# Two Mamba layers as one run of 32 chunks, with weights exchanged on the way and the carries' constants copied by DMA

## What is computed

```python
def _block(x, in_w, cw, cb, xp_w, dtw, dtb, a_log, dp, ow):
    xb, z = jnp.split(jnp.einsum('bld,ed->ble', x, in_w), 2, axis=-1)
    xb = silu(conv of 4 taps over xb + cb)
    dbc = jnp.einsum('ble,re->blr', xb, xp_w)          # delta (16), Bm (16), Cm (16)
    delta = softplus(jnp.einsum('blr,er->ble', delta, dtw) + dtb)
    dA = jnp.exp(delta[..., None] * -jnp.exp(a_log))
    mi = delta[..., None] * Bm[:, :, None, :] * xb[..., None]
    def scan_fn(carry, inp):
        h, v = carry
        v = 0.6 * v + mi_t
        h = dA_t * h + v
        return ((h, v), einsum('ben,bn->be', h, C_t))
    y = (ys + dp * xb) * silu(z)
    return jnp.einsum('ble,de->bld', y, ow)
for i in range(2):
    x = x + _block(_rmsnorm(x, norm_w[i]), in_proj_w[i], ...)
```

## Time and profile before

| | |
|---|---|
| runs | 4176.25 us median of 3 (4171.02 to 4178.72) |
| profiled execution | 4180.98 us, its span 4179.2 us |
| mean granted TensorE clock | 0.863 of full speed |
| Mamba's two layers, first load to last residual | 974.7 to 3408.3 us of the span |
| first to last scan | 1065.0 to 2172.9 us, and 2283.1 to 3396.4 us |

### The profile page before, as it was taken

How to read it: one execution, slowest core, us unless ns; L and a number is a source line. 1 busy time by engine, 2 the same in 40 slices (tenths; PEclk the granted TensorE clock), 3 DMA queues, 4 the chain that set the end, 5 groups by cost and what they waited for, 6 DMA issues and landing times. The chain is left out here.

```text
span 4179.2 us, 94211 instructions
## 1 busy us (share of the span) xinstructions
PE 3158.1 (76%) x31116; PEld 2527.5 (60%) x31117; DVE 2746.0 (66%) x4803; ACT 2019.3 (48%) x4522; POOL 1996.0 (48%) x1170
## 2 busy tenths in 40 slices
PE   6888886991778888787864787787878753799980
PEld 4455554660666666676762676676667653688870
DVE  3444442325788888888874888887888877555445
ACT  1211211222676777677644777676676743133320
POOL 0100100001577777777661767767686766221116
PEclk8788886995889999999986899999999875799995
DMA  1000000002223232323221222323232324111113
GB/s 53 0 0 0 0 0 22 0 0 67 68 56 83 54 84 55 81 57 82 54 56 49 67 72 56 83 54 82 55 80 58 79 89 165 54 45 48 48 42 109
DMA packets 151643, 230.75 MB, mean 55 GB/s; under 512 B 25106, under 2 KB 83890, under 8 KB 149556
## 3 DMA queue, kind: packets, MB, share of 16 engines
q1 hardware_dynamic: 143156, 202.30, 18.1%
q0 software_dynamic: 8064, 23.08, 1.9%
HBM read 119.99 MB, written 23.59 MB: 34 GB/s over the span
## 5 line engine op out<-in xcount | busy, mean ns | idle before, releaser
L890 POOL TENSOR_TENSOR m_hc<-m_h,m_Cb 128x1024 f32<-128x1024 f32 x512 | 1230.1, 2410 | 627.4 <-DVE m_h L1014 366.6
L1014 DVE TENSOR_TENSOR_SCAN m_h<-m_dA,m_hlast,m_bank 128x256 f32<-128x256 f32 x2048 | 1344.8, 725 | 192.1 <-PE m_bank L1329 127.8
L1308 PE MATMUL m_bank<-ident,m_hc 128*128 128x128 f32 x4096 | 687.6, 297 | 298.1 <-POOL m_hc L890 297.8
L1152 ACT ACTIVATE m_dA<-m_delta,m_rate 128x256 f32<-128x256 f32 x2048 | 894.1, 500 | 15.7 <-issue 14.2
L1327 PE MATMUL m_bank<-m_M,m_U 128*128 128x64 bf16 x8192 | 688.4, 198 | 115.3 <-DMA m_U<-m_clo 92.1
L1327 PEld LDWEIGHTS m_bank<-m_M,m_U 128*128 128x128 bf16 x8192 | 615.9, 102 | 203.2 <-issue 141.3
L1329 PE MATMUL m_bank<-m_M,m_U 112*128 112x64 bf16 x8192 | 688.2, 198 | 5.2 <-issue 5.2
L1308 PEld LDWEIGHTS m_bank<-ident,m_hc 128*128 128x128 f32 x4096 | 473.9, 151 | 317.1 <-issue 316.8
L1329 PEld LDWEIGHTS m_bank<-m_M,m_U 112*128 112x128 bf16 x8192 | 588.2, 101 | 72.3 <-issue 51.1
L1995 ACT ACTIVATE x_h<-x_bank,x_b 128x256 f32<-128x256 f32 x320 | 134.4, 471 | 286.8 <-PE x_bank L1941 271.4
L1901 POOL DMA_INDIRECT x_x_in<-xn_rows,r_from_row x80 | 91.0, 1137 | 350.7 <-PE x_bank L1925 302.7
(11 more groups left out here) (279 smaller groups left out, 5990.2 us busy)
## 6 DMA issues: line engine op xcount, KB each, us to landing
m_Cb<-m_c_rows SPq DMA_DIRECT2D x256, 256.0 KB, 3.3
m_M<-m_Mhi SPq DMA_DIRECT2D x128, 256.0 KB, 4.3
m_M<-m_Mlo SPq DMA_DIRECT2D x64, 256.0 KB, 3.6
m_U<-m_Uhi SPq DMA_DIRECT2D x128, 128.0 KB, 3.1
y_rows<-x_y SPq DMA_DIRECT2D x40, 256.0 KB, 2.1
m_U<-m_Ulo SPq DMA_DIRECT2D x64, 128.0 KB, 3.1
g_stage<-in_e_w SPq DMA_DIRECT2D x8, 1024.0 KB, 5.2
o_stage<-in_e_w SPq DMA_DIRECT2D x16, 512.0 KB, 4.6
```

Source lines behind the costliest of these rows:

```text
L890: nc.gpsimd.tensor_tensor(hc[:, hc_slot[n]], h[:, n % RING], Cb[:, g % 2, n % NG, :].unsqueeze(1).broadcast_to([P, KI, CM]), ALU.mult).the ...
L1014: nc.vector.tensor_tensor_scan(h[:, n % RING, m, :], dA[:, n % RING, m, :], VB[(n % 2) * 2 + g][:, (m % 2) * CM:(m % 2 + 1) * CM], hlast[: ...
L1152: nc.scalar.activation(dA[:, n % RING, m, :], delta[:, par, m, :], ACT.Exp, scale=rate[:, m, n:n + 1]).then_inc(s["da_done"], 1)
L1308: last = nc.tensor.matmul(Y[half][:, m * P:(m + 1) * P], hc[:, hc_slot[n], m, half * P:(half + 1) * P], net.ident[:], is_transpose=True, s ...
```

## The change

`mamba_phase` runs once, for both layers: 32 chunks, where chunk 16 is the first of layer 1.

- Small per-layer weights (norm, taps, bias, rates, skip and its diagonals) are kept for both layers. The large ones (`w_in`, 1 MB, `w_xp`, `w_dt`) have one place: SyncE loads those of layer 1 in chunk 14, after its sixth spread and the placements of u, once the last products with the old ones are counted; TensorE waits for them (`swapped`) ahead of the input product of chunk 16. `w_out` is exchanged likewise in chunk 16, and waited for in chunk 17.
- Where layer 1 begins, the conv history is zeroed on GpSimd instead of copied (chunk 16), the last h of chunk 15 is kept as zeros on ScalarE, and VectorE fills the velocity's carry with zeros in chunk 15.
- Chunks 14 to 17 stand between two loops, written out on all engines. The slots' numbers go into a table `AT`, with the values that the code had.
- The six loads of the constants come first and on a semaphore of their own. VectorE makes one place of M2 and no longer waits for the other loads to do so; one transfer from SyncE's queue copies it to the other seven. TensorE waits for the copy ahead of the first velocity, and for the diagonals (now eight, a third `const_done`) ahead of its clearing.
- Each tap on VectorE adds one to a counted semaphore `tap_done` and waits for the tap before it there, instead of on a plain semaphore that was cleared at each chunk's start; likewise `joined` for the sum of delta.

```diff
-def mamba_phase(net, layer, xm):
+def mamba_phase(net, xm):
...
-        LOADS = 18 * 16
+        LOADS = (6 + 5 * LAYERS) * 16
+        LAST = LAYERS * NCM
...
-                for t, key in ((norm, "norm"), (w_in, "in"), (conv, "conv"), (conv_b, "conv_b"), (w_xp, "xp"),
-                               (rate, "alog"), (skip, "skip"), (w_out, "out")):
-                    sp.dma_start(t[:], dram[f"m{layer}_{key}"]).then_inc(s["loaded"], 16)
-                sp.dma_start(w_dt, dram[f"m{layer}_dt"]).then_inc(s["loaded"], 16)
+                for part in range(3):
+                    at = SUB + part * NS
+                    sp.dma_start(Mf[at:at + NS], dram["decay"][SUB:SUB + NS]).then_inc(s["const_loaded"], 16)
+                    sp.dma_start(Gf[at:at + NS, 0], dram["carry_on"]).then_inc(s["const_loaded"], 16)
+                for t, key in ((norms, "norm"), (convs, "conv"), (conv_bs, "conv_b"), (rates, "alog"), (skips, "skip")):
+                    for layer in range(LAYERS):
+                        sp.dma_start(t[:, layer], dram[f"m{layer}_{key}"]).then_inc(s["loaded"], 16)
+
+                def swap(layer, sem):
+                    sp.dma_start(w_in[:], dram[f"m{layer}_in"]).then_inc(sem, 16)
+                    sp.dma_start(w_xp[:], dram[f"m{layer}_xp"]).then_inc(sem, 16)
+                    sp.dma_start(w_dt, dram[f"m{layer}_dt"]).then_inc(sem, 16)
+
+                swap(0, s["loaded"])
                 sp.dma_start(carry_of[:], dram["carry_of"]).then_inc(s["loaded"], 16)
                 for half in range(2):
                     sp.dma_start(decay[half * SUB:(half + 1) * SUB, :], dram["decay"][0:SUB, 0]).then_inc(s["loaded"], 16)
...
+                sp.dma_start(w_out[:], dram["m0_out"]).then_inc(s["out_swapped"], 16)
+                sp.wait_ge(s["const_done"], 1 + 2)
+                rows = M2[SUB:KV].rearrange("p a j n t -> p (a j) (n t)")
+                sp.dma_start(rows[:, 1:], rows[:, 0:1].broadcast_to([KV - SUB, 2 * NSUB - 1, NS * SUB])
+                             ).then_inc(s["spread_done"], 16)
...
+                        if swapping and g == SPREAD["u"]:
+                            sp.wait_ge(s["in_psum"], 1 + NCM * 4)
+                            sp.wait_ge(s["xp_psum"], 1 + NCM)
+                            sp.wait_ge(s["dt_psum"], 1 + NCM * 2)
+                            swap(1, s["swapped"])
+                        if isinstance(c, int) and c == NCM and g == SPREAD["u"]:
+                            sp.wait_ge(s["out_psum"], 1 + NCM + 1)
+                            sp.dma_start(w_out[:], dram["m1_out"]).then_inc(s["out_swapped"], 16)
...
+                        if isinstance(q, int) and q == NCM:
+                            nc.gpsimd.memset(xpre[:, :, 0:TAPS - 1], 0.0).then_inc(s["halo_done"], 1)
...
             def _(dve):
-                dve.wait_ge(s["loaded"], LOADS)
                 dve.wait_ge(s["setup"], 1 + 1)
-                for m in range(KI):
-                    nc.vector.scalar_tensor_tensor(dskip[:, m, :], net.ident[:], skip[:, m:m + 1], net.ident[:],
-                                                   ALU.mult, ALU.mult)
+                dve.wait_ge(s["const_loaded"], 6 * 16)
...
-                    for j in range(NSUB):
-                        nc.vector.tensor_copy(M2[SUB:SUB + 2 * NS, par, j], Mf[SUB:SUB + 2 * NS])
-                        nc.vector.tensor_copy(M2[SUB + 2 * NS:KV, par, j], Mf[SUB + 2 * NS:KV])
+                nc.vector.tensor_copy(M2[SUB:SUB + 2 * NS, 0, 0], Mf[SUB:SUB + 2 * NS])
+                nc.vector.tensor_copy(M2[SUB + 2 * NS:KV, 0, 0], Mf[SUB + 2 * NS:KV])
...
-                for par in range(2):
-                    for j in range(NSUB):
-                        nc.vector.tensor_tensor(M2[SUB + 2 * NS:KV, par, j], Mf[SUB + 2 * NS:KV],
-                                                M2[SUB + 2 * NS:KV, par, j], ALU.subtract)
+                nc.vector.tensor_tensor(M2[SUB + 2 * NS:KV, 0, 0], Mf[SUB + 2 * NS:KV],
+                                        M2[SUB + 2 * NS:KV, 0, 0], ALU.subtract)
...
+                dve.wait_ge(s["loaded"], LOADS)
+                for layer in range(LAYERS):
+                    for m in range(KI):
+                        i = nc.vector.scalar_tensor_tensor(dskip[:, layer, m, :], net.ident[:], skips[:, layer, m:m + 1],
+                                                           net.ident[:], ALU.mult, ALU.mult)
+                i.then_inc(s["const_done"], 1)
...
+                        if k == 0:
+                            dve.wait_ge(s["pre_done"], 1 + q * 2 + g + 1)
+                        else:
+                            dve.wait_ge(s["tap_done"], 1 + q * len(TAP_ORDER) + TAP_ORDER.index((g, k - 1)) + 1)
...
+                    if isinstance(c, int) and c == NCM - 1:
+                        nc.vector.memset(U2[SUB:KV, 0, 0], 0.0).then_inc(s["moved_next"], 3 * 16)
...
+                    nc.scalar.copy(hlast[:, n, :], none[:] if ending else h[:, n % RING, :, CM - 1]).then_inc(s["hlast_done"], 1)
...
-                pe.wait_ge(s["const_done"], 1 + 2)
+                pe.wait_ge(s["const_done"], 1 + 3)
...
+                            if isinstance(q, int) and q == NCM:
+                                pe.wait_ge(s["swapped"], 3 * 16)
...
+                            if isinstance(t, int) and t in (0, NCM + 1):
+                                pe.wait_ge(s["out_swapped"], 16 * (1 + t // NCM))
...
+                pe.wait_ge(s["spread_done"], 1 + 16)
                 velocity(0, 0, 0, 0)
...
-    for layer in range(LAYERS):
-        net.run(lambda n: mamba_phase(n, layer, net.x_all))
+    net.run(lambda n: mamba_phase(n, net.x_all))
```

More of the change, by code:

```diff
@@ L657 @@
 RING, LEAD, OFF, NG, NHC = 4, 2, 10, 2, 3
[L660 removed]
+AT = {
+    "square_x": 0, "root": 1, "xr": 3, "xT_mm": 4, "xT": 5, "halo": 6, "in": (6, 7, 8, 9, 10, 11, 12, 13), "pre": (8, 10),
+    "tap00": 11, "tap01": 11, "tap02": 11, "tap10": 13, "tap11": 13, "tap12": 13, "z": 15, "xb": 15, "xp_mm": 17, "xp": 18,
+    "bc_mm": 19, "bs": 20, "dt_mm": 21, "gf": 21, "mf0": 21, "far": 22, "ghi": 22, "clamp": 23, "exp": 23, "mhi": (23, 27), "sq": 24,
+    "mlo0": 24, "mf1": 24, "near": 25, "ln": 26, "series": 26, "delta": 27, "glo": 27, "u": 28, "mlo1": 30, "uT_mm": 30, "uhi": 31, "ulo": 32,
+    "carry_mm": 33, "chi": 34, "clo": 35,
+    "gate": 3, "gT_mm": 4, "gT_copy": 5, "skip_mm": 5, "out_mm": (7, 8), "residual": 9}
+SPREAD = {"keep": 2, "high": 4, "low": 6, "u": 6, "carries": 7}
+TAP_ORDER = sorted(((g, k) for g in range(2) for k in range(TAPS - 1)), key=lambda t: (AT[f"tap{t[0]}{t[1]}"], t))
+def mamba_phase(net, xm):
     nc = net.nc
     dram = net.dram
[L664 removed]
+    nm = lambda t: f"m_{t}"
     with ExitStack() as ctx:
         sb = lambda t, shape, dt=F32: net.sb(ctx, nm(t), shape, dt)
[L667 removed]
+        norms, convs, conv_bs = sb("norm", [P, LAYERS, KD]), sb("conv", [P, LAYERS, KI, TAPS]), sb("cb", [P, LAYERS, KI])
+        w_in = sb("in", [P, KD, 2 * DI])
         w_xp = sb("xp", [P, KI, RANK + 2 * NS])
         w_dt = sb("dt", [SUB, DI])[2 * NS:2 * NS + RANK + 1, :]
[L670 removed]
+        rates, skips, w_out = sb("rate", [P, LAYERS, KI, NS]), sb("skip", [P, LAYERS, KI]), sb("out", [P, KI, D])
+        none = sb("none", [P, KI])
         decay, carry_of = sb("decay", [P, SUB]), sb("carry_of", [P, TM, NSUB])
@@ L1057, in _, with head @@
                 act.wait_ge(s["floor_done"], 1 + 2)
-                def head(q, par, at):
-                    tiles = [xm[:, (q + 1) * TM + j, :] for j in range(TM)]
-                    if at == 0:
+                def head(q, par, at, layer):
+                    norm, conv, conv_b = norms[:, layer], convs[:, layer], conv_bs[:, layer]
+                    tiles = [xm[:, (q - layer * NCM + 1) * TM + j, :] for j in range(TM)]
+                    if at == AT["square_x"]:
                         for j in range(TM):
@@ L1152, in decays, with keep_last, slots @@
                         nc.scalar.activation(dA[:, n % RING, m, :], delta[:, par, m, :], ACT.Exp,
-                                             scale=rate[:, m, n:n + 1]).then_inc(s["da_done"], 1)
-                def keep_last(c, n):
+                                             scale=rates[:, layer, m, n:n + 1]).then_inc(s["da_done"], 1)
+                def keep_last(c, n, ending):
                     act.wait_ge(s["scan_done"], 1 + AHEAD + (c * NS + n + 1) * KI)
                     act.sem_inc(net.carrier, 1)
-                    nc.scalar.copy(hlast[:, n, :], h[:, n % RING, :, CM - 1]).then_inc(s["hlast_done"], 1)
-                def slots(c, par, more, more2):
+                    nc.scalar.copy(hlast[:, n, :], none[:] if ending else h[:, n % RING, :, CM - 1]).then_inc(s["hlast_done"], 1)
+                def slots(c, par, more, more2, layers, ending=False):
+                    now, after, beyond = layers
                     for n in range(NS):
@@ L1335, in late, with slots @@
```

(2 more changed lines are left out.)

330 lines of the change are left out of this document (174 added, 156 removed).

## The result

The changed kernel takes 4077.02 us, the median of four runs (4063.26 to 4081.8); the kernel before took 4173.64 us in the runs beside it (four, 4168.46 to 4178.72). The ratio is 0.9759, with a 95% interval of 0.9741 to 0.9777. The forecast was 4077.3 us. The profiled execution took 4081.8 us, its span 4079.9, against 4179.2 before: 99.3 us less in the spans, where the working had 99.0.

A forecast was written before the change was run, and what follows sets the result against it. No engine is full: each chunk is a ring of dependent work over five engines, with stages setting the end. Seam -82.9, start -18.2, exchange +1.9, semaphores +0.2 give -99.0 us: 4176.25 becomes 4077.3 us, range 4062 to 4096.

The forecast's parts named there:

- a band of 8.4: 28 untouched periods could come out anywhere between the two layers' means, +-0.30 x 28 = 8.4 us.
- The seam: Between gates of layer 0's chunk 14 and layer 1's chunk 1: 296.14 us become three periods, 213.2; gain 82.9 us.
- chunks 14, 15, 16 and 17 are ordinary chunks: Step of the seam's term: three periods lie there, each charged at the two layers' mean, 71.07 us.
- the prediction's signs of being right: Among them: the period between gates stays at 70 to 72.5 us through chunks 14 to 17.
- The start of layer 0: Constants leave the path ahead of TensorE's first transposes, which come at 994.0 instead of 1012.16; gain 18.2 us.
- the landing of the last load: At layer 0's start, the input weight lands at 987.6 and the three small loads behind it at 988.0.
- rival B: At layer 0's start the constants' part gives nothing, as loads or copy land late; +18.2 us, 4095.5; chance 0.07.
- The exchange: SyncE's weight loads in chunks 14 and 16 delay carries and TensorE's input product; +1.9 us, from 0 to 5.1.
- rival A: Exchange loads and placements queue up fully, TensorE stands 6.7 us; 7.9 us more than forecast, 4085.2; chance 0.10.
- The slack that the prediction gave GpSimd: 5.12 us of GpSimd's waiting right behind chunk 14's last spread, to take up the spread's part of the delay.
- Rival C: Slower than before: 224 tap waits on a running count, each above 0.44 us, eat the gain; chance 0.02.
- The copy: Transfer of constants, 688 KB, issued near 986, landing near 993, some 50 us before TensorE needs it.

The follow-up runs named there:

- e_port: The changed kernel, with GpSimd's product of state 7 in written-out chunks waiting for VectorE's sum of delta; 4065.23 us, ratio 0.9737.
- e_const_old: The changed kernel, one run of 32 chunks, but with layer 0's constants made as before, their loads last; 4095.53 us, ratio 0.9821.
- e_start: The changed kernel with a looser start: engines wait for loads and diagonals only where they first use them; 4076.48 us, ratio 0.9766.
- e_no_swap: The changed kernel without the exchange of weights, layer 1 computing with layer 0's large weights; 4077.91 us, ratio 0.9775.
- e_swap_late: The changed kernel with chunk 14's three weight loads issued after the last spread and the carries; 4091.54 us in a single run.
- e_port_before: The kernel before, with GpSimd's product of state 7 in written-out chunks waiting for delta (the sum and two maxima); 4178.34 us, ratio 1.0012.

## Why the prediction was right, and where it was off

- **The total** is right to 0.3 us, and its two large steps are right, but the closeness is partly luck. In the traces the seam and the start gave 5.2 us less than their terms, and the stretches that the change does not touch happened to be 5.3 us shorter; half of that, 2.6 us, lies in the periods for which the prediction had a band of 8.4. In the medians the gain is 96.6 us and not 99.0: the forecast started from 4176.25, and the kernel before took 4173.64 beside the changed one, whose own four runs spread over 18.5 us. The terms of the forecast's band, added up, give 4065 to 4092, and 4061 to 4096 with the 4 us between runs, where it says 4064 to 4090.
- **The seam** was forecast by its ends and three ordinary periods, and that is what happened, with 77.4 us where 81.0 were forecast. The step that was mis-sized is "chunks 14, 15, 16 and 17 are ordinary chunks", charged with the mean of 71.07 of mostly looped chunks. They are written out, and three of such chunks with the long sum cost 4.1 us more (218.72 against 214.65 in e_port, with the exchange in both). So one of the prediction's signs of being right failed: of the four periods of chunks 14 to 17 (74.78, 70.48, 73.46, 72.44) two lie outside 70 to 72.5. Its mean over the untouched chunks held (71.0 us over 27 periods). The trace of before could have warned in part: the six long sums stood there, and layer 0's first period of 72.38 lay ahead of the stretch that gave the mean. But its second, 72.11, was in the mean, and layer 1's first two, with the same long sum, took 70.39 and 71.07.
- **The start of layer 0**: 18.2 forecast, 16.6 measured from the first load. The order of events was as described; the mis-sized term is the landing of the last load, 15.0 us after the first issue (at 988.58) where 13.3 were worked out. e_const_old gives back 18.5 us in the median and refutes rival B. The 19 us of the first transposes were 20.9.
- **The exchange**: +1.9 forecast, within 0 to 5.1. Chunk 14's period is 2.7 us shorter without it (72.09, against 74.78 in the changed kernel and 74.42 and 73.54 in e_const_old and e_start), so the size is right, as far as single periods can tell. The wait at the input product was 4.07 us where the sign of being right was 2 to 3, and GpSimd's for the spread grew from 0.44 to 3.29: the transfers do stand behind one another, as rival A had it. The slack that the prediction gave GpSimd was not used: its next wait is 5.71 us, and 5.61 in e_no_swap. The two waits overlap in time, and chunk 14 is 2.7 us longer with both. The Trainium skill (DMA: Bandwidth & Descriptors, section Queues, rings and completion order) has such an order of descriptors on one engine; these two waits agree with it, but no run here tells it from transfers that share the engines. A price of A's size (1.9 + 7.9 = 9.8 us) came only where the loads were put later: chunk 14's period is 9.0 us longer in e_swap_late than without the exchange.
- **Rival C**, the taps' waits on a running count: the first fourteen periods of layer 0, twelve of them looped, take the same time as before (992.21 us, -0.14), with six such waits in each chunk. Refuted.
- **The copy** was taken to land near 993 and landed at 993.7, with the cover of some 50 us that the prediction had given it. That is luck in part: it was issued at 984.56, not near 986, and took 9.1 us from there, where some 7 had been taken.

## What to carry to other kernels

A phase boundary inside a long pipeline costs the drain, the constants, and above all a head with nothing beside it; price it by the distance between two like events on both sides, less the ordinary periods that would lie there, and count periods of chunks that run in the same kind of code. Where chunks written out by hand are slower than the loop's, compare the durations of single instructions in both before looking for waits: here an instruction that was 2 us longer beside another engine's, which was then 1 us shorter, was a matter of order, and a wait of the less urgent engine set it. Such a wait must be on exactly the instruction that has to go first, since one that holds the other engine a little longer leaves what follows as late as it was (u in e_port_before).

## What the runs showed of the hardware

VectorE's sum of two operands in SBUF and GpSimd's product did not share their time: an order that differed by 0.3 us decided whether the sum took 1.28 us or 3.24, and the product 2.34 or 3.37.

TensorE's granted clock went with that order. In the second chunk TensorE stops in mid-chunk, for 5.13 us in the changed kernel and for 6.69 in e_port, where GpSimd's product waits for the sum; up to there the clock is 1.00 in both. After the longer stop it then works with one gap above 0.3 us (0.41) up to the transposes of u; after the shorter one it stands three times more, for 0.8, 1.0 and 1.2 us, the last for u. In both the clock falls to the lower of its two levels (0.50, 1.2 of 2.4 GHz) in the stop. In the changed kernel it is still there 12.2 us after the work goes on; in e_port it is back at 1.00 after 4.9 us (a row of the timeline, then stretches with length, the five engines, granted clock, DMA share, GB/s; the changed kernel, then e_port):

```profile
1161.13 1.09 PE L1375 MATMUL m_bank<-ident,m_hc 128*128 128x128 f32 x4 [5.13 <-POOL m_hc L936]
1161.10:1173.30 12.20, 9.22 (x86) 8.16 (x87) 11.00 (x17) 7.19 (x20) 10.31 (x6) 0.50 0.52 124
```

```profile
1156.73 0.66 PE L1377 MATMUL m_bank<-ident,m_hc 128*128 128x128 f32 x2 [6.69 <-POOL m_hc L936]
1156.70:1161.60 4.90, 4.61 (x44) 4.12 (x44) 4.79 (x8) 2.65 (x9) 4.90 (x4) 0.50 0.83 189
1161.60:1182.00 20.40, 15.34 (x228) 13.23 (x229) 14.42 (x23) 15.14 (x42) 17.04 (x11) 1.00 0.48 128
```

So the long sum goes with a longer time at the lower level. The clock alone does not make the period, though. In e_port_before, where the sum is short but the stop is 8.0 us and u as late as before, the same chunk has a mean clock of 0.93 and still takes 72.45 us:

```profile
1147.95:1220.40 72.45, 56.41 (x744) 47.82 (x743) 58.66 (x90) 50.77 (x117) 50.06 (x27) 0.93 0.27 67
```

How much of a late sum reaches the period through the clock and how much through the later u is not shown.
